# Expert routing in a fused attention and mixture-of-experts kernel: totals added on TensorE, dropped choices in an upper half of the table, one record per choice

## The reference

```python
raw = softmax(logits)                                  # per token, over E = 8 experts
idx1 = argmax(raw);  m1 = one_hot(idx1);  gate1 = sum(raw * m1)
rest = raw * (1 - m1)
idx2 = argmax(rest); m2 = one_hot(idx2);  gate2 = sum(rest * m2)
p1 = cumsum(m1, tokens) - m1                           # place within the expert
m1 = m1 * (p1 < C)                                     # C = 256: later tokens are dropped
p2 = cumsum(m2, tokens) - m2 + sum(m1, tokens)         # second choices queue behind the first
m2 = m2 * (p2 < C)
# the token goes to expert idx1 at place p1 with gate1, and to idx2 at p2 with gate2;
# every place computes (gelu(x @ w0) * (x @ w1)) @ wo, and out adds gate * result
```

## Time and profile before

| what | value |
|---|---|
| median of three timed runs | 1648.45 us |
| their lowest and highest | 1641.49 and 1649.46 us |
| time of the profiled execution | 1658.51 us |
| its span, first to last instruction | 1656.8 us |
| mean granted TensorE clock in it | 0.993 |
| PE busy | 1620.5 us (98%) |
| PEld busy | 1396.0 us (84%) |
| DVE busy | 939.8 us (57%) |
| ACT busy | 762.3 us (46%) |
| POOL busy | 506.1 us (31%) |

### The profile page before, as it was taken

The page is one execution under the profiler, slowest core; times in us unless marked ns, Lnnn a source line. Parts: engine busy times, 40 slices in busy tenths (PEclk is TensorE's granted clock), DMA queues, the critical chain, the costliest instruction groups (busy, mean ns, idle before and its releaser), DMA issues.

```text
span 1656.8 us, 22948 instructions
## 1 busy us (share of the span) xinstructions
PE 1620.5 (98%) x8450; PEld 1396.0 (84%) x8450; DVE 939.8 (57%) x1955; ACT 762.3 (46%) x1389; POOL 506.1 (31%) x433
## 2 busy tenths in 40 slices
PE   7999899799999999999999999999999999999998
PEld 6888788688888888888888888888888888888887
DVE  7999754345644564447544654466445644475453
ACT  5777545234433453336333543345334533453333
POOL 2156566563222222222222222222222222222211
PEclk9999999899999999999999999999999999999999
DMA  7553121025422342225211522243223422351211
GB/s 169 160 160 122 53 80 45 13 41 120 86 38 37 81 93 37 39 43 124 39 36 36 135 38 39 39 109 71 39 39 82 93 36 38 64 109 33 36 13 13
DMA packets 193848, 110.94 MB, mean 67 GB/s; under 512 B 96008, under 2 KB 189640, under 8 KB 193736
## 3 DMA queue, kind: packets, MB, share of 16 engines
q1 hardware_dynamic: 165064, 75.37, 18.1%
q0 software_dynamic: 28672, 34.10, 12.8%
HBM read 60.11 MB, written 34.61 MB: 57 GB/s over the span
## 4 chain that ended last, share of the span: by engine, by line
PE 79%; DVE 6%; issue 4%; ACT 3%; SPq 3%; POOL 2%; DMA 2%; another core or an unknown queue 1%; POOLq 0%; ACTq 0%; DVEq 0%
PE bank L1691 23%; PE bank L1714 21%; PE bank L1730 14%; PE bank L1732 8%; PE bank L1503 7%; DVE y L1440 2%; PE bank L1556 1%; PE bank L1705 1%; SPq L509 1%; ACT hhi L922 1%; DVE hlo L1443 1%; SPq L426 1%; POOL slots L658 1%; POOL out L726 1%
## 5 line engine op out<-in xcount | busy, mean ns | idle before, releaser
L726 POOL DMA_INDIRECT out<-xring,slot_records x128 | 215.4, 1683 | 858.1 <-DVE xring L1410 792.9
L922 ACT ACTIVATE hhi<-y 128x512 fp32r<-128x512 f32 (+1 forms) x349 | 220.8, 633 | 508.7 <-DVE y L1440 427.6
L1730 PE MATMUL bank<-wo,hhi 128*128 128x512 f32 (+1 forms) x1276 | 443.7, 385 | 2.0 <-DVE hlo L1443 1.8
L1440 DVE TENSOR_TENSOR y<-bank,sig 128x512 f32<-128x512 f32 x320 | 220.9, 690 | 334.1 <-PE bank L1714 300.8
L1732 PE MATMUL bank<-wo,hlo 128*128 128x256 f32 x1396 | 382.2, 274 | 0.1
L1443 DVE TENSOR_TENSOR hlo<-y,hhi 128x512 fp32r<-128x512 f32 (+1 forms) x349 | 241.6, 692 | 243.9 <-ACT hhi L922 237.6
L912 ACT ACTIVATE sig<-bank 128x512 f32<-128x512 f32 x320 | 189.6, 593 | 209.2 <-PE bank L1691 181.9
L1730 PEld LDWEIGHTS bank<-wo,hhi 128*128 128x128 f32 (+1 forms) x1276 | 239.1, 187 | 50.5 <-DVE hlo L1443 4.0
L1732 PEld LDWEIGHTS bank<-wo,hlo 128*128 128x128 f32 x1396 | 261.6, 187 | 9.2 <-issue 0.8
L1691 PE MATMUL bank<-xThi,whi 128*128 128x512 f32 (+1 forms) x704 | 217.0, 389 | 7.4 <-issue 3.5
L1691 PE MATMUL bank<-xTlo,whi 128*128 128x512 f32 (+1 forms) x704 | 213.2, 383 | 0.0
(11 more groups left out here) (147 smaller groups left out, 1730.6 us busy)
## 6 DMA issues: line engine op xcount, KB each, us to landing
stage<-in_L_ffn_w_kernel SPq DMA_DIRECT2D x160, 128.0 KB
rows<-rows SPq DMA_DIRECT2D x448, 32.0 KB, 1.9
stage<-in_L_ffn_wo_kernel SPq DMA_DIRECT2D x80, 128.0 KB
xring<-in_L_attn_x SPq DMA_DIRECT2D x16, 512.0 KB
out<-xring SPq DMA_DIRECT2D x16, 512.0 KB
x_rows<-rows SPq DMA_DIRECT2D x16, 512.0 KB
slots<-records,sloti POOLq DMA_INDIRECT x128
rows<-x_rows,slot_records POOLq DMA_INDIRECT x128
```

What stands on the lines that cost most here:

```text
L726: pool.indirect_dma_start(out_rows, bass.IndirectOffsetOnAxis(idx, 0), ysb[:, t % 2, j, :], None, compute_op=ALU.add).then_inc(added, 16)
L922: act.activation(h_high(e, t, hc)[0:n, :], hf[0:n, hc % 2, :], ACT.Copy).then_inc(h_hi, 1)
L1440: dve.tensor_tensor(hf[0:n, hc % 2, :], up_value(e, t, hc)[0:n, :], gel[0:n, hc % 2, :], ALU.mult).then_inc(mul_done, 1)
L1730: pe.matmul(lines(yb[j][:, :]), high, lines(wo[0:n, hc, :, :].rearrange("p s c -> p (s c)")), start=hc == 0, stop=end, skip_group_check=True)
```

## The change

`count` no longer makes the ninth tile. It has 1 + 7 + 8 = 16 matmuls in place of 9: the eight new ones add each tile's first-choice mask, multiplied by ones, to the places of the second choice in all eight tiles. The places of the second choice then contain the uncapped total of the first. `place` has 6 operations in place of 12. The table has an upper half of the size of the first; a dropped choice gets the same slot number plus `NSLOT`, and the dump rows are gone. Each choice has a record of its own with one gate, so `choose` writes the gates straight into the records, and its sixth operation has the wait for the ring (`wait_scattered`) that `place` had. `gates`, `expert_no` and `gate_done` are gone: ACT and DVE read the gate in the slot record, and wait for `records_loaded`. POOL's constants change: four iotas fill the source rows in place of two, the cleared record buffer is twice as large, and the iota of `dump` and two memsets are gone. Both choices still cost a record of 32 bytes for each token.

```diff
-    GT1, GT2, EX1, TOK, SRC = range(5)
+    GATE, TOK, SRC = range(3)
-    slots = nc.dram_tensor("slots", [NSLOT + 4 * S, REC], F32, kind="Internal").ap()
+    slots = nc.dram_tensor("slots", [2 * NSLOT + 2 * S, REC], F32, kind="Internal").ap()
-        mask = sb("mask", [P, 2, TILES + 1, E], BF16)
+        mask = sb("mask", [P, 2, TILES, E], BF16)
-        records = sb("records", [P, RING, TILES, REC])
+        records = sb("records", [P, RING, 2, TILES, REC])
...
             def choice(g, n):
+                gate = records[:, g.ring(RING), k, :, GATE]
                 elif n in (5, 11):
-                    dve.reduce_max(gate[:, k, :], p[:, :, :], AXX).then_inc(choose_chain, 1)
+                    if n == 5:
+                        for h in range(2):
+                            wait_scattered(dve, g, h)
+                    dve.reduce_max(gate, p[:, :, :], AXX).then_inc(choose_chain, 1)
...
             def placing(g, n):
                 if n == 0:
                     wait(dve, counted, g, 1, 1)
-                    dve.tensor_scalar(cnt1[:, :], tot, float(CAP), None, ALU.min).then_inc(place_chain, 1)
+                    dve.tensor_tensor(pos[:, :, :, :], cum, mask[:, :, :, :], ALU.mult).then_inc(cum_read, 1)
                 elif n == 1:
-                    dve.tensor_tensor(pos[:, 0, :, :], cum[:, 0, 0:TILES, :], first_mask, ALU.mult)
-                elif n == 2:
-                    wait(dve, place_chain, g, 7, 1)
-                    dve.tensor_tensor(pos[:, 1, :, :], cum[:, 1, 0:TILES, :],
-                                      cnt1[:, :].unsqueeze(1).to_broadcast([P, TILES, E]),
-                                      ALU.add).then_inc(cum_read, 1)
-                elif n == 3:
                     wait(dve, cum_read, g, 1, 1)
-                    dve.tensor_tensor(pos[:, 1, :, :], pos[:, 1, :, :], second_mask, ALU.mult).then_inc(place_chain, 1)
-                elif n == 4:
-                    wait(dve, place_chain, g, 7, 2)
                     dve.reduce_sum(psel[:, :, :].rearrange("p k t -> p (k t)"),
                                    pos[:, :, :, :].rearrange("p k t e -> p (k t) e"), AXX).then_inc(place_chain, 1)
-                elif n == 5:
...
+                elif n == 2:
+                    wait(dve, place_chain, g, 2, 1)
+                    dve.tensor_scalar(dropped[:, :, :], psel[:, :, :], float(CAP), float(NSLOT), ALU.is_ge, ALU.mult)
+                elif n == 3:
                     dve.scalar_tensor_tensor(out=slotf[:, :, :], in0=top[:, :, :], scalar=-float(ESLOTS),
                                              in1=psel[:, :, :], op0=ALU.mult, op1=ALU.add).then_inc(place_chain, 1)
...
+                elif n == 4:
+                    wait(dve, place_chain, g, 2, 2)
+                    dve.scalar_tensor_tensor(out=sloti[:, g.ring(RING)].rearrange("p k t -> p (k t)"),
                                              in0=slotf[:, :, :].rearrange("p k t -> p (k t)"),
...
+                                             scalar=float(E * ESLOTS + g.value * CAP),
+                                             in1=dropped[:, :, :].rearrange("p k t -> p (k t)"),
+                                             op0=ALU.add, op1=ALU.add)
                 else:
-                    dve.tensor_scalar(row[:, :, TOK].bitcast(I32), tokid[:, :], float(g.value * S), None,
+                    dve.tensor_scalar(records[:, g.ring(RING), :, :, TOK].bitcast(I32),
+                                      tokid[:, :].unsqueeze(1).to_broadcast([P, 2, TILES]), float(g.value * S), None,
                                       ALU.add).then_inc(routed, 1)
...
-                    act.wait_ge(gate_done, FT * e + t + 1)
+                    act.wait_ge(records_loaded[t], 16 * (e + 1))
...
                             act.activation(part[:, j, :], yb[j][:, D:2 * D], ACT.Copy,
-                                           scale=gslot[:, t % 2, j:j + 1]).then_inc(part_done, 1)
+                                           scale=slot_records[:, t, j, GATE:GATE + 1]).then_inc(part_done, 1)
...
-                        if hc == PREPARE[0] and t < FT - 1:
-                            gates(e, t + 1)
-                        elif hc == PREPARE[0] and not last:
-                            in_gate.begin(Turn(e), FT)
-                            in_gate.link(dve.tensor_scalar(expert_no[:, :], expert_no[:, :], 1.0, None, ALU.add))
-                            gates(e + 1, 0)
...
                 pe.matmul(cum, before[:, :], mask[:, :, :, :], start=True, stop=False)
                 for t in range(TILES):
-                    rest = TILES - t
-                    last = pe.matmul(cum[:, :, t + 1:TILES + 1, :], ones[:, :],
-                                     mask[:, :, t:t + 1, :].to_broadcast([P, 2, rest, E]),
+                    rest = TILES - t - 1
+                    if rest:
+                        pe.matmul(cum[:, :, t + 1:TILES, :], ones[:, :],
+                                  mask[:, :, t:t + 1, :].to_broadcast([P, 2, rest, E]), start=False, stop=False)
+                    last = pe.matmul(cum[:, 1, :, :], ones[:, :], mask[:, 0, t:t + 1, :].to_broadcast([P, TILES, E]),
                                      start=False, stop=t == TILES - 1)
```

More of the change, by code:

```diff
@@ L603, in _ @@
             pool.memset(ones[:, :], 1.0)
-            pool.memset(records[:, :, :, :], 0.0).then_inc(consts_raw, 1)
+            pool.memset(records[:, :, :, :, :], 0.0).then_inc(consts_raw, 1)
             pool.memset(zero[:, :], 0.0)
@@ L608, in _ @@
             pool.iota(fill[:, :, :, SRC].bitcast(I32), pattern=[[0, 2], [0, FJ]], base=2 * S, channel_multiplier=0)
-            for r in range(0, RING, 2):
-                pool.iota(records[:, r:r + 2, :, SRC].bitcast(I32), pattern=[[S, 2], [P, TILES]], base=0,
+            for r in range(RING):
+                pool.iota(records[:, r, :, :, SRC].bitcast(I32), pattern=[[0, 2], [P, TILES]], base=S * (r % 2),
                           channel_multiplier=1)
@@ L659, in scatter @@
                             slots[:, :], bass.IndirectOffsetOnAxis(sloti[:, g.ring(RING), k, t:t + 1], 0),
-                            records[:, g.ring(RING), t, :], None).then_inc(scattered[t // HT][g.parity], 16)
+                            records[:, g.ring(RING), k, t, :], None).then_inc(scattered[t // HT][g.parity], 16)
             def gather(e, t):
@@ L1154, in placing @@
                                              in0=slotf[:, :, :].rearrange("p k t -> p (k t)"),
-                                             scalar=float(E * ESLOTS + g.value * CAP), in1=dump[:, g.parity],
-                                             op0=ALU.add, op1=ALU.subtract).then_inc(place_chain, 1)
-                elif n == 8:
-                    wait(dve, place_chain, g, 7, 6)
-                    dve.scalar_tensor_tensor(out=slotf[:, :, :], in0=row_gates, scalar=0.0, in1=slotf[:, :, :],
-                                             op0=ALU.not_equal, op1=ALU.mult).then_inc(place_chain, 1)
-                elif n == 9:
-                    wait(dve, place_chain, g, 7, 7)
-                    dve.tensor_tensor(sloti[:, g.ring(RING)].rearrange("p k t -> p (k t)"),
-                                      slotf[:, :, :].rearrange("p k t -> p (k t)"), dump[:, g.parity], ALU.add)
-                elif n == 10:
-                    dve.tensor_scalar(row[:, :, EX1], top[:, 0, :], -1.0, float(E), ALU.mult, ALU.add)
-                else:
-                    dve.tensor_scalar(row[:, :, TOK].bitcast(I32), tokid[:, :], float(g.value * S), None,
+                                             scalar=float(E * ESLOTS + g.value * CAP),
@@ L1180, in projection_weights @@
                                   ALU.subtract).then_inc(wq_lo, 1)
-            def gates(e, t):
-                dve.wait_ge(records_loaded[t], 16 * (e + 1))
-                record = slot_records[:, t]
-                dve.scalar_tensor_tensor(out=gsel[:, 0, :], in0=record[:, :, EX1], scalar=expert_no[:, :],
-                                         in1=record[:, :, GT1], op0=ALU.is_equal, op1=ALU.mult)
-                in_gate.begin(Turn(e), t)
-                in_gate.link(dve.scalar_tensor_tensor(out=gsel[:, 1, :], in0=record[:, :, EX1],
-                                                      scalar=expert_no[:, :], in1=record[:, :, GT2],
-                                                      op0=ALU.not_equal, op1=ALU.mult))
-                dve.tensor_tensor(gslot[:, t % 2, :], gsel[:, 0, :], gsel[:, 1, :], ALU.add).then_inc(gate_done, 1)
             def prepare(e, t, k):
@@ L1313, in step @@
                 if Dg:
-                    place(back2, 0, 4)
+                    place(back2, 0, 1)
                 outputs(i, 1, 0)
@@ L1320, in step @@
                 if Dg:
-                    place(back2, 4, 5)
+                    place(back2, 1, 2)
                 if A:
@@ L1324, in step @@
                 if Dg:
-                    place(back2, 5, 7)
+                    place(back2, 2, 4)
```

(16 more changed lines are left out.)

36 lines of the change are left out of this document (6 added, 30 removed).

## The result

The changed kernel takes 1649.7 us (median of 20 runs, 1646.2 to 1654.5) where the kernel before takes 1645.0 (median of 20, 1641.5 to 1651.2). The ratio is 1.0028, with a 95% interval of 1.0019 to 1.0037: 4.7 us slower. I had said 1647.8, 0.6 us faster than the 1648.45 that three runs of before had given.

The account below looks back on a forecast made before the run. The prediction took TensorE to bound nearly everywhere. Count at +1.6 us and gates at -2.2 us, all else 0, gave -0.6 us, so 1648.45 became 1647.8 us; the range for 8 in 10 was 1638 to 1656 us.

Parts of the forecast that it names:

- The count: TensorE's count in the routing steps: seven more matmuls, eight times, at 0.2 us each time, +1.6 us.
- Rival (c): Count on TensorE: the added matmuls do not overlap, since all add to the same columns; 1657.1 us, chance 0.03.
- `place`: VectorE in the routing steps: six of twelve operations go, freeing 5.2 us over six steps, none reaching the end; 0.
- The idle time ahead of the second scan: VectorE after place in a routing step: a sign, idle time up from 0.67 to over 1 us.
- Rival (a): Routing steps: VectorE bounds them after all, so another 5.2 us come off; 1642.6 us, chance 0.07.
- The gates: Expert tile t = 3, hc = 5: 0.66 us leaves VectorE's stream before five TensorE waits; -2.2 us, bounds 0 and 4.6.
- The waits at line 1679: TensorE's waits for VectorE's hidden chunks, 320 to 1600 us: a sign, below 0.5 us together, from 2.2.
- The waits moved, the constants: Ring wait before choose's sixth operation, record-load waits on ACT and VectorE, and POOL's constants at the start: each 0.
- Landings: POOL's record scatters: as many as before, only the place of dropped records changes; 0.
- a sign of being wrong: A TensorE wait for POOL or a DMA that was not there before would show the prediction wrong.
- Rival (d): Standstill in every run, or dropped records in scattered rows slowing POOL's landings: up to 10.1 us, 1657.9 us, chance 0.07.
- Rival (b): Whole span: the changed kernel meets less of the unexplained standstill, about 10 us of TensorE idle time; 1638 us, chance 0.13.

Follow-up runs that it names:

- totals alone: Before with only the new count and a place of nine operations, its first four merged into one multiply: 1650.13 us, ratio 1.0027.
- records-alone kernel: Before with only a record for each choice and without the gates operations in the experts: 1647.06 us, ratio 1.0006.
- upper-half kernel: Before with only dropped choices sent to an upper half of the table in place of dump rows: 1646.02 us, ratio 0.9997.
- every eight: Before, but from step 7 on POOL waits for a landing after every eight record scatters in place of four: 1639.02 us, ratio 0.9962.
- the dose: Before with 7 or 21 matmuls adding a mask of zeros in each count: 1651.07 us (1.0040) and 1650.74 us (1.0035).
- the second trace of the changed kernel: The changed kernel run once more, unedited: 1648.57 us, ratio 1.0023 to before.
- the two runs of before with 112 instructions: Before with 112 semaphore increments at TensorE's start: 1657.35 us, 1646.3 less the shift; or 56 small matmuls and their weight loads there: ratio 0.9986.
- the loosened kernels: Before and the changed kernel, each with POOL's landing wait after every eight scatters from step 7 on: 1639.02 and 1641.32 us.
- padded changed kernel: The changed kernel with 72 matmuls of 8 x 8 ahead of the first weights: ratio 0.9996 on the standstill chip, 1644.8 us (0.9998) elsewhere.
- both edits: Before with landing waits after every eight scatters and the first record load moved behind step 5: 1679.45 us (standstill chip), 1636.13 us, ratio 0.9946, elsewhere.

## Why the prediction was wrong, point by point

**The count.** Right in mechanism and size. TensorE in order, step 3 of the changed kernel, against the earlier trace rows:

```profile
99.73 0.22 PE L1510 MATMUL bank<-mask,before 128*128 128x128 bf16 x1
99.78 0.21 PE L1515 MATMUL bank<-mask,ones 128*128 128x112 bf16 x1
...
100.20 0.22 PE L1517 MATMUL bank<-mask,ones 128*128 128x64 bf16 x2
100.25 0.69 PE L1450 MATMUL bank<-xThi,wThi 128*128 128x512 f32 x2
```

Sixteen take 0.52 us, 33 ns each, where nine took 0.35. Eight times 0.17 is 1.4 us (forecast 1.6). Rival (c), no overlap, is out. The Trainium skill ("TensorE: Matmul & The Clock Gate", section "Back-to-back issue gap") gives 81 ns for a pair of weight load and matmul at 128 columns. For these narrower ones, 16 to 128 columns wide, that is too much: the trace has 33 ns.

**`place`.** Nothing came of it that can be measured: the changed kernel (1.0028, and 1.0023 again) is not apart from the totals alone (1.0027), which have nine operations in place of twelve. The idle time ahead of the second scan, which I said would go from 0.67 to over 1 us, is 0.16 in step 3:

```profile
105.06 1.28 DVE L1004 TENSOR_TENSOR_SCAN y<-sig,y,bank 128x512 f32<-128x512 f32 x1 [0.16 <-PE bank L1450]
```

The 0.67 us that I built on belonged to that one execution. Without the standstill VectorE has no idle time there at all in a before-like trace, so it is nearer to bounding than I said. Rival (a) is out all the same, with a step of 25.6 us after and 25.4 before.

**The gates.** Wrong is the term of -2.2 us, the step that 0.66 us of VectorE at hc = 5 lies ahead of TensorE's waits and is gained. Alone it was measured at +0.7 us (1647.06 against 1646.34), and its interval leaves 2.2 us out. The waits at line 1679 came to 4.1 us in six places, not below 0.5, and the records-alone kernel has 3.6. What ends there is the staging of the next weights: VectorE's split waits for ACT's, and that for a DMA. The row from the changed kernel, for tile 3 of expert 2:

```profile
736.69 0.69 DVE L1166 TENSOR_TENSOR wlo<-stage,whi 128x512 fp32r<-128x512 f32 x1 [3.20 <-ACT wo L883]
```

What VectorE no longer does, it waits longer: 25.9 us in all for these splits between 320 and 1640 us, against 21.4 in the upper-half kernel, which still has the gates. I had named this bound (a DMA ends these waits: 0) and yet taken all of the 2.2 us. With 0 in this place the sum would have been slower, by 1.6.

**The waits moved, the constants.** Right: the sixth operation of `choose`, with the ring's wait, never idles in the trace, in any of the eight groups.

**Landings.** Here the prediction failed. "Its place changes: 0" was right for the reason I weighed, scattered rows. But I let POOL's chain off the path because no row named it, in a profile whose standstill hid it. The wait of TensorE for POOL and a DMA, which I had named as a sign of being wrong, was there, but it was there before the change too. The sum priced the added matmuls by their own time and put everything that they move at 0. Rival (d) had the right member, slower landings, with a wrong cause. The runs show in its place that POOL's chain of landings ends the drain and holds TensorE up by 2 to 6 us, with 3 to 7 us at the lower clock in most traces, and that the added matmuls cost 4.7 us where their work is 1.4. The remaining 3.3 us, for which the sum had nothing, come with the totals (1.0027 alone). That the added instructions shift the loads of code against POOL's chain is my reading of them, in part contradicted.

**The number.** 1647.8 lies only 1.9 us below the measured 1649.7, and that is luck: the base of 1648.45, from three runs, was 3.4 us above the median of twenty. The forecast of the difference was off by 5.3 us: 2.2 for the gates, 3.3 for what came with the totals beside their work, less 0.2 for the count. Rival (b), less of the standstill, is out: the timed runs of before, at 1645.0, did not have most of it.

**How sure that is.** Shown: the chain bounds (every eight); the totals bring the loss; the loss does not follow the dose; adding instructions that take no time in the steps takes the loss away (by ratios from different chips), but not where the chain is loosened, where it takes nothing. Seen twice to the packet, at scatter 96 of two traces, but not isolated: that a load of code makes a landing late. Argued only: that this is what the 3.3 us are. Against it stand the second trace of the changed kernel, which lost time without a late landing there, and the two runs of before with 112 instructions. A rival that nothing here excludes is that the added instructions shift all streams against each other, and that TensorE's waits elsewhere, those for staged weights in the experts among them, and the stretches at the lower clock carry a part. Open: why 112 instructions in before cost 1.4 us and, on the other chip, nothing, and not 3 to 7; where the remaining distance of 2.3 us between the loosened kernels lies beyond the count's 1.4 us (the two ratios' intervals overlap); and what the standstills are, which on one chip add 12 us to before and to the padded changed kernel, and 43 us to before with both edits.

## What to carry to other kernels

Before a wait table is trusted to say what is not on the path, subtract the standstills of the profiled execution, or take a trace without them: a chain that makes TensorE wait 3.5 to 5.1 us in each trace of the changed kernel and its parts was invisible behind 13 us of additional idle time. A serial chain of issue and landing on one queue is a bound to be counted by itself (issues times spacing, plus landings), even where its engine is 31% busy. Price a wait of TensorE with the clock that it is granted behind it. And when an edit costs more than its work, vary the dose: here the cost did not grow with it, which points to position rather than work, and taking the chain that bounds off the path brought 6 to 8 us whatever the cause.

## What the runs showed of the hardware that I had not expected

- Loads of code go over the same DMA engines as data, 16 KB at a time, mostly 0.9 to 1.4 us each. In two traces a record scatter's last two packets started when such a load had ended, and it landed up to 1.8 us later (3.75 in place of 1.95 us of wait).
- Behind a wait of TensorE of 3.4 to 6.2 us at the end of the drain, or already within it, the granted clock was at its lower level for 3.4 or 6.8 us, in every trace that had one; behind 2.1 us it stayed at the upper level once and behind 2.2 us it fell once.
- A semaphore increment in TensorE's stream took 0.15 us (144 of them put the first matmul at 23.1 us, 112 at 18.3); 72 matmuls of 8 x 8 with their weight loads took 1.95 us, 27 ns each.
- The landing of a scatter of 128 rows of 32 bytes kept POOL for 1.4 us when the queues were quiet, and for 3.6 to 5.2 us under the stores of 219 to 223 us, when the DMA engines were busy without a gap.
- The same program differs by chip: before takes 1645 to 1646 us on three of them and 1658 on a fourth, through standstills that no record explains. The mean granted clock is lower there too, 0.992 to 0.998 in the runs of before against 0.996 to 1.000. The edits that won on one chip (0.9946) lost there (1.0118).
